# A fused attention and mixture kernel whose feed-forward pieces stand six slots sooner in the written order

## The chip, the cores and the metric

The kernel runs on one core of one Trainium2 chip. The metric is the device time of one execution in microseconds (us). Five engines work side by side, each through its own instructions in order: TensorE (PE in the profile), VectorE (DVE), ScalarE (ACT), GpSimd (POOL) and SyncE (SP), which here only starts transfers. They meet through semaphores.

## The reference

For 32 sequences of 256 tokens with 256 channels, a gated cross attention is added to `x` and then a gated feed-forward part:

```python
x = x + tanh(g_xattn) * xattn(layernorm(x), ctx, ctx, W, b, mask)    # 16 heads, 77 keys, causal and padded
x = x + tanh(g_ffn)   * ffn(layernorm(x), ...)
# ffn: shared = swiglu(flat @ w_in.T) @ w_out.T
#      h      = swiglu(flat @ w1.T); routed = sum over e of (h * w_se[:, e]) @ w2[e].T
#      w_se: of 2 groups the likelier, in it the 2 best of 4 experts (softmax, top 2)
```

## The kernel before

**Two phases.** Phase one computes attention, the second layer norm, the router and the shared feed-forward part, and it sorts tokens by pair of experts: an indirect transfer from GpSimd (L1473) writes each token's record into a table. Phase two gathers the tokens of each pair, tile by tile, and multiplies them with the experts' weights.

**One written order.** `phase_one()` returns a list of entries (name, index, part). Every engine walks through this same list and issues what is its own of each entry, so that the list fixes the order on all queues. The list is made by a loop over steps i = 0 to 34, each of 12 slots. In step i the stages of four batches overlap: the key/score work of batch i-1 (`max`), scores and values of batch i-2, projection and second norm of batch i-3, first norm of batch i. A batch is one sequence of 256 tokens; two batches make a chunk.

**Feed-forward pieces.** The shared part of a chunk is cut into 24 pieces `ffn`, and two of them stand at the end of every odd slot. Pieces 0 to 15 make the hidden layer (L712, three matmuls of 512 columns each), four pieces for each of the four blocks fc of 128 hidden channels. At the second piece of a block ScalarE computes a tanh (L932) and VectorE a product (L1248, "u"); at the fourth VectorE computes the block (L1256, "f"). At the second piece of the *next* block ScalarE rounds f (L853, `gh`) and GpSimd computes the rest f - gh (L1375, `gl`). Pieces 16 to 23 multiply `gh` and `gl` with the output weights (L729, six matmuls of 256 columns each); piece 16 + fc waits for `gl` of block fc. After pieces 19 and 23 VectorE adds the result to x (L1266, `res`) and SyncE stores it (L510).

The wait of the second half of the pieces, and what GpSimd does at an entry `moments` (the inverse root of a variance and a scaled mean, four small instructions L1382, L1384, L1431, L1433, the first of which waits for VectorE's statistics L989 and L993):

```python
if hb == 0:
    e.wait_ge(s["gl"], 4 * b + fc + 1)      # TensorE, pieces 16 to 19
...
root(0, b)                                   # GpSimd at "moments": waits for VectorE, then L1382, L1384
```

**Routing steps.** With each piece one routing step of VectorE (L1032 to L1131) is issued, from the step on at which the chunk's logits are there; steps 30 to 37 of a route are the eight table writes of GpSimd (L1473). A route takes 38 steps and starts in slot 5 of every fourth step. So VectorE has routing steps 8 to 19 in steps 8, 12, ..., 28 and GpSimd has its table writes at the end of step 9, 13, ... and in steps 10, 14, ..., 30.

**Banks.** `take()` gives each use of PSUM a bank of a ring, and the use waits until the one before it in that bank has been read. `max`, `scores` and `att` share two pairs of banks (ring P): the first `scores` of a step (L615) waits until VectorE has read the `att` of the step before (L1212), the k-th `max` (L586) until VectorE has reduced the one before (L1192).

**Transfers of x.** SyncE loads x of a batch for the residual (L500) in slot 11, behind the copies of `queries` (L487), and GpSimd adds the bias (L1449) in slot 2 of the next step; VectorE's projection (L1221) waits for that.

Of the kernel before, what the change touches and what calls it, by code (L numbers as in the profile page):

```python
# [59 lines left out]
def phase_one():  # L60

    order = []
    at = {"ffn": 0, "r": 0, "k": 0}
# [8 lines left out]
    def ffn(routes):  # L72

        order.append(("ffn", pieces[at["ffn"]] // 24, pieces[at["ffn"]] % 24))
        at["ffn"] += 1
        for _ in range(routes):
            route()
# [14 lines left out]
    for i in range(NB + 3):  # L92
        slots = [[] for _ in range(12)]

        def put(b, stages):
            if 0 <= b < NB:
                for slot, name, k in stages:
                    slots[slot].append((name, b, k))

        if i % 2 == 1:  # L100
            put(i - 4, ((2, "logits", 0), (5, "logitsT", 0)))
            if i < NB + 1:
                put(i - 4, ((6, "store_x2", 0),))
        put(i - 2, ((1, "scores", 0), (3, "scores", 1), (5, "scores", 2), (5, "values", 0), (7, "scores", 3), (8, "values", 1),
                    (5 if i < 6 else 11, "load_x1", 0), (11, "att", 0)))

        put(i - 1, ((0, "max", 0), (0, "max", 1), (0, "max", 2), (0, "max", 3), (3, "maxT", 0)) if i < 6 else
            ((0, "max", 0), (2, "max", 1), (4, "max", 2), (6, "max", 3), (9, "maxT", 0)))

        put(i - 3, ((2, "bias", 0), (1, "attT", 0), (4, "proj", 0), (7, "norm2", 0), (10, "x2T", 0)) if i < NB + 2 else  # L110
            ((1, "bias", 0), (1, "attT", 0), (3, "proj", 0), (5, "norm2", 0), (7, "x2T", 0), (9, "logits", 0), (10, "logitsT", 0)))
        put(i, ((2, "norm", 0), (6, "xT", 0), (10, "queries", 0)))
        put(i + 1, ((8, "moments", 0),))

        put(i, ((1, "keys", 0), (3, "keys", 1)))
        if i == 0:
            slots[5].append(("init", 0, 0))
            slots[8].append(("vau", 0, 0))
            slots[9].append(("own", 0, 0))
            slots[11].append(("load_kv", 1, 0))  # L120
        if i == 1:
            slots[8].append(("own", 1, 0))
            slots[10].append(("gates", 0, 0))
            slots[11].append(("masks", 1, 0))
        if i == 2:
            slots[4].append(("zeros", 0, 0))
            slots[6].append(("pads", 1, 0))
            slots[11].append(("load_weights", 0, 0))

        if i == 2:  # L130
            slots[8].append(("weights", 0, 0))
            slots[10].append(("weights", 1, 0))
        if i in (4, 5):
            slots[9].append(("weights", i - 2, 0))

        if i == 5:
            slots[2].append(("weights_low", 2, 0))
        if i == 6:
            slots[1].append(("weights_low", 3, 0))
        if i % 2 == 1 and i + 1 < NB:  # L140
            slots[11] += [("kv", i // 2 + 1, 0), ("vau", i // 2 + 1, 0)]
        if i % 2 == 0 and 0 < i < NB - 2:
            slots[8].append(("load_kv", i // 2 + 1, 0))
        if i == NB:
            slots[0].append(("load_w1", 0, 0))
        if i == NB + 1:
            for k in range(4):
                slots[2 * k + 2].append(("split", k, 0))
        if i == NB + 2:
            order.append(("wide", 0, 0))  # L150
            for k in range(4):
                slots[2 * k + 2].append(("hid", 0, k))
        for slot in range(12):
            for name, b, k in slots[slot]:
                order.append((name, b, k))
                if name == "logitsT":
                    logits.add(b // 2)
            if slot == 3 and i + 2 < NB:
                order.append(("load_x", i + 2, 0))
            while at["ffn"] < (12 * (i - 5) + slot - 9) // 2 * 2:  # L160
                ffn(1 if i < NB - 1 else 3)
            if i == NB + 2 and slot == 4:
                held = None
        if 1 <= i < 5:
            order.append(("clear", i - 1, 0))
# [31 lines left out]
def build(nc, A, out):  # L197
    ctx = ExitStack()
    with ctx:
        order = phase_one()  # L200
        names = (

# [1352 lines left out]
```

How the kernel before makes its waits and increments, by code:

```python
        def sync(e):  # L414
            def load_kv(b):
                h = b % 2
                if b >= 1:
                    e.wait_ge(s["klo"], b)
                e.dma_start(kf[:, :, :], A["ctxT"][b].rearrange("p (a k) -> p a k", k=K)).then_inc(
                    s[f"kf{h}"], 16)
                if b >= 1:
                    e.wait_ge(s["vau"], b)
                e.dma_start(vf[:, :, :], A["ctx_1024"][b * G:b * G + G].rearrange("b k d -> k b d")).then_inc(
                    s[f"vf{h}"], 16)
# [4 lines left out]
                for r, t in enumerate((khi, klo, khi)):  # L429
                    for j in range(2):
                        o = 32 * r + 16 * j
                        dst = Kst[o:o + 16, h, j, :, :, :].rearrange("p q a k -> p (q a k)")
                        e.dma_start(dst.bitcast(F), t[64 * j:64 * j + 64, :, :].bitcast(F)).then_inc(s[f"kd{h}"], 16)
            for stage_, b, k in order:
                h = b % 2
                if stage_ == "load_x":
                    if b >= 2:
                        e.wait_ge(s["xn"], b - 1)
                    e.dma_start(xt[:, h, :, :], A["x"][b].rearrange("(t p) d -> p t d", p=P)).then_inc(
                        s[f"xi{h}"], 16)
                elif stage_ == "consts":
# [11 lines left out]
                    e.dma_start(wt_s, A["WT"].rearrange("(c p) n -> p c n", p=P)).then_inc(s["w2"], 16)  # L454
                elif stage_ == "masks" and b == 1:
                    e.wait_ge(s["ks1"], 2)
# [568 lines left out]
                def after():  # L1026
                    e.wait_ge(*chain[0])
```

## Time and profile before

| | us |
|---|---|
| runs: median of three (lowest, highest) | 1164.55 (1162.37, 1165.7) |
| profiled execution, first to last instruction | 1154.6 |
| TensorE busy in it | 1105.4 |
| VectorE, GpSimd, ScalarE busy | 820.0, 519.1, 470.4 |
| steps 6 to 31 of phase one | from 91.2 to 633.0 |

The profiled execution's own time outside its span is not recorded; the span lies 9.95 us under the median of the runs, which is launch and end. The clock of TensorE was at its upper level (2.4 GHz, 1.0 in the profile) for nearly all of the span, mean 0.987. A row of the timeline gives start, length, engine, line, operation, what it writes and reads, and in brackets how long its engine was idle before it and for whom.

### The profile page before, as it was taken

What the parts mean: (1) busy time and instruction counts of PE and PEld (TensorE: products, weight loads), DVE (VectorE), ACT (ScalarE), POOL (GpSimd) and SP (SyncE); (2) the same over time, 40 slices, a digit from 0 to 9 for tenths busy, and PEclk for the clock granted to TensorE, in tenths of its full rate; (3) what the DMA queues carried; (4) which work ended last, traced back from release to release, by engine and by line L of the source; (5) the groups of instructions that cost most, each with busy time, mean ns of one, the idle gap of its engine ahead of it and who ended that gap; (6) DMA issues with size and microseconds to landing.
All of it is one profiled execution on the core that took longest, in us unless ns stands there. A gap on an engine that the chain in (4) does not pass through costs nothing.

```text
span 1154.6 us, 22482 instructions
## 1 busy us (share of the span) xinstructions
PE 1105.4 (96%) x7475; PEld 917.9 (80%) x7475; DVE 820.0 (71%) x1778; ACT 470.4 (41%) x722; POOL 519.1 (45%) x647
## 2 busy tenths in 40 slices
PE   5789999999999999999999899999999899999997
PEld 3557888787887788788788677788888788888886
DVE  7757686786786876876877576557544588888886
ACT  4565556545555555555654432223221111111111
POOL 5334447347356346456454523100000666666564
PEclk9989999999999999999999999999999899999999
DMA  8984647656665765764755311587662554555451
GB/s 158 242 191 80 145 98 128 132 118 107 136 125 93 148 131 115 123 141 102 118 117 109 70 46 38 199 263 236 209 211 93 162 160 150 164 162 157 147 177 65
DMA packets 106163, 160.65 MB, mean 139 GB/s; under 512 B 28828, under 2 KB 70718, under 8 KB 106048
## 3 DMA queue, kind: packets, MB, share of 16 engines
q1 hardware_dynamic: 94276, 121.18, 46.0%
q0 software_dynamic: 11776, 38.03, 10.6%
q8 instruction: 65, 1.06, 0.4%
q14 instruction: 46, 0.38, 0.1%
HBM read 75.24 MB, written 52.10 MB: 110 GB/s over the span
## 4 chain that ended last, share of the span: by engine, by line
PE 72%; DVE 10%; issue 8%; POOL 6%; ACT 2%; DMA 1%; POOLq 0%; ACTq 0%; DVEq 0%
PE ps L767 15%; PE ps L814 12%; PE ps L712 8%; PE ps L816 6%; PE ps L729 6%; PE ps L632 4%; PE ps L620 3%; PE ps L663 3%; PE ps L799 3%; POOL tab_dram L1473 2%; PE ps L586 2%; PE ps L590 2%; PE ps L615 1%; PE ps L697 1%; PE ps L686 1%
## 5 line engine op out<-in xcount | busy, mean ns | idle before, releaser
L814 PE MATMUL ps<-regr,gh 128*128 x600 | 221.5, 407 | 0.1
L891 ACT ACTIVATE Pt<-ps,pbias 77x1024 f32<-77x1024 f32 x128 | 141.4, 1105 | 107.4 <-PE ps L620 106.2
L816 PE MATMUL ps<-regr,gl 128*128 x600 | 170.0, 283 | 0.0
L814 PEld LDWEIGHTS ps<-regr,gh 128*128 128x128 f32 x600 | 113.8, 190 | 23.6 <-issue 0.5
L981 ACT ACTIVATE gh<-ps 128x512 fp32r<-128x512 f32 x75 | 44.8, 599 | 204.5 <-PE ps L799 204.5
L1192 DVE TENSOR_REDUCE mneg<-ps 128x8 f32<-128x616 f32 x128 | 100.5, 792 | 19.7 <-PE ps L590 19.6
L816 PEld LDWEIGHTS ps<-regr,gl 128*128 128x128 f32 x600 | 114.2, 190 | 0.0
L712 PE MATMUL ps<-x2h,winh 128*128 128x512 f32 x256 | 110.6, 432 | 0.5 <-DVE OHR L1096 0.5
L1375 POOL TENSOR_TENSOR gl<-gf,gh 128x512 fp32r<-128x512 f32 x64 | 82.5, 1290 | 50.4 <-ACT gh L853 50.1
L712 PE MATMUL ps<-x2h,winl 128*128 128x512 f32 x256 | 101.5, 396 | 0.0
L712 PE MATMUL ps<-x2l,winh 128*128 128x512 f32 x256 | 101.2, 395 | 0.0
L1449 POOL TENSOR_TENSOR x<-x,regf 128x512 f32<-128x512 f32 x32 | 41.1, 1284 | 130.4 <-DMA x<-in_x 130.4
L1361 POOL DMA_INDIRECT yt<-y_dram,Pt x73 | 75.5, 1035 | 53.2 <-PE ps L816 42.7
L1499 POOL DMA_INDIRECT out<-ot,Pt x75 | 77.6, 1035 | 41.3 <-issue 27.9
L1287 DVE SCALAR_TENSOR_TENSOR Pt<-Pt,ps 128x512 f32<-128x512 f32 x64 | 44.0, 688 | 69.0 <-ACT Pt L975 67.8
L975 ACT ACTIVATE Pt<-ps 128x512 f32<-128x512 f32 x64 | 38.3, 598 | 129.8 <-PE ps L767 129.8
L620 PE MATMUL ps<-regr 100*77 100x256 f32 x512 | 87.9, 295 | 0.0
L767 PE MATMUL ps<-regr,x2h 128*128 128x512 f32 x256 | 82.4, 396 | 0.0
L1424 POOL TENSOR_TENSOR regr<-regr,own 128x616 fp32r<-128x616 f32 x64 | 78.4, 1226 | 5.7 <-ACT regr L862 5.4
L1473 POOL DMA_INDIRECT tab_dram<-rec,slot x64 | 64.7, 1011 | 26.7 <-issue 13.3
L1320 DVE SCALAR_TENSOR_TENSOR ot<-ps,Pt,ot 128x256 f32<-128x256 f32 x150 | 72.6, 484 | 5.4
L632 PE MATMUL ps<-Pt,regf 77*32 77x256 f32 x1024 | 69.5, 389 | 6.1 <-ACT Pt L891 6.1
(201 smaller groups left out, 2681.7 us busy)
## 6 DMA issues: line engine op xcount, KB each, us to landing
regr<-regr SPq DMA_DIRECT2D x96, 256.0 KB, 5.9
y_dram<-Pt SPq DMA_DIRECT2D x64, 256.0 KB, 2.2
regf<-in_x SPq DMA_DIRECT2D x32, 256.0 KB, 2.9
x<-in_x SPq DMA_DIRECT2D x32, 256.0 KB, 7.2
y_dram<-res SPq DMA_DIRECT2D x32, 256.0 KB, 2.2
regr<-regr SPq DMA_DIRECT2D x96, 77.0 KB, 6.9
x_dram<-x2h SPq DMA_DIRECT2D x14, 512.0 KB, 3.0
x_dram<-x2l SPq DMA_DIRECT2D x14, 512.0 KB, 3.8
```

The source lines that it names most:

```text
L620: m = e.matmul(bk[0:K, j * S:(j + 1) * S], Kst[:, ks, j, p % 4, 2 * g + p // 4, :], Xs[:, h, p % 4, p // 4, :], start=False, stop=j == 1, ...
L632: m = e.matmul(bk[32 * j:32 * j + 32, q * S:(q + 1) * S], Vau[:, ks, g, n, :], Pt[0:K, n, :], start=True, stop=True)
L712: m = e.matmul(bk[:, :], w[:, cc, off:off + P], x[:, b % 2, cc, :], start=cc == 0 and n == 0, stop=cc == 1 and n == 2)
L767: i = e.matmul(bk[:, :], x[:, cc, k * P:(k + 1) * P], w[:, cc, half * 512:half * 512 + 512], start=n == 0, stop=n == 5)
L814: e.matmul(o, gh2[:, k % 3, fc, :], w2v[:, bass.ds(val, 1), fc, :, :].rearrange("p o h d -> p (o h) d"), start=fc == 0, stop=False, skip_g ...
L816: m = e.matmul(o[:, 0, :], gl2[:, k % 3, fc, :], w2v[:, bass.ds(val, 1), fc, 0, :].rearrange("p o d -> p (o d)"), start=False, stop=fc == ...
L891: e.activation(Pt[0:K, 4 * k:4 * k + 4, :].rearrange("k (n j) t -> k n (j t)", n=2), bank_of["sc", b, k][0:K, :, :], ACT.Exp, bias=pbias[: ...
L1192: e.tensor_reduce(mneg[:, h, t, :].rearrange("p (j q c) -> p c j q", j=2, c=2)[:, c], bank_of["mm", b, k][:, :, 0:4 * K].rearrange("p q (f ...
L1375: e.tensor_tensor(gl[:, fc, :], gf[:, n % 2, :], gh[:, fc, :].bitcast(F), ALU.subtract).then_inc(s["gl"], 1)
L1424: e.tensor_tensor(Kbd[:, b % G, k, :, :], khi[:, b % G * 2 + k, :].bitcast(F).unsqueeze(1).broadcast_to([P, 8, K]), own8[:, :].unsqueeze(2 ...
L1473: e.indirect_dma_start(tab, bass.IndirectOffsetOnAxis(ap=slot[:, j:j + 1], axis=0), rec[:, j, :], None, bounds_check=NC * NT - 1, oob_is_e ...
L1499: e.indirect_dma_start(out.rearrange("b s d -> (b s) d"), bass.IndirectOffsetOnAxis(ap=rt[:, k, 0:1].bitcast(I32), axis=0), ot[:, k % 8, : ...
```

## The change

The number of pieces that must have been placed by slot `slot` of step `i` is `(12 * (i - 5) + slot - 9) // 2 * 2` before and `(12 * (i - 5) + slot - 3) // 2 * 2` after. The first two pieces stand in slot 5 of the sixth step (i = 5) instead of slot 11, and each piece after them six slots sooner. The routing steps are tied to pieces, but a route starts when its logits are in the list, which has not moved.

```diff
             if slot == 3 and i + 2 < NB:
                 order.append(("load_x", i + 2, 0))
-            while at["ffn"] < (12 * (i - 5) + slot - 9) // 2 * 2:
+            while at["ffn"] < (12 * (i - 5) + slot - 3) // 2 * 2:
                 ffn(1 if i < NB - 1 else 3)
             if i == NB + 2 and slot == 4:
                 held = None
```

How a chunk c lies in the slots of its steps (odd step 5 + 2c, even step 6 + 2c and so on; each slot named holds two pieces):

| | slots and pieces |
|---|---|
| before | odd 11: 0, 1; even 1: 2, 3; 3: 4, 5; 5: 6, 7; 7: 8, 9; 9: 10, 11; 11: 12, 13; next odd 1: 14, 15; 3: 16, 17; 5: 18, 19; 7: 20, 21; 9: 22, 23 |
| after | odd 5: 0, 1; 7: 2, 3; 9: 4, 5; 11: 6, 7; even 1: 8, 9; 3: 10, 11; 5: 12, 13; 7: 14, 15; 9: 16, 17; 11: 18, 19; next odd 1: 20, 21; 3: 22, 23 |

**GpSimd in an even step without table writes.** The rows run from slot 1 to the end of the step; L1424 are the keys, L1449 the bias, L1382 and L1384 the roots, L1375 is `gl`. Before:

```order
L1424 TENSOR_TENSOR regr<-regr,own 128x616
L1375 TENSOR_TENSOR gl<-gf,gh 128x512
L1382 TENSOR_SCALAR ve<-mv 128x2
L1384 TENSOR_TENSOR rs<-ve,mhalf 128x2
L1442 TENSOR_TENSOR first<-pad,caus 128x77
L1375 TENSOR_TENSOR gl<-gf,gh 128x512
L1382 TENSOR_SCALAR ve<-mv 128x2
L1384 TENSOR_TENSOR rs<-ve,mhalf 128x2
L1431 TENSOR_TENSOR mr<-mv,rs 128x2
L1433 TENSOR_SCALAR mr<-mr 128x2
L1375 TENSOR_TENSOR gl<-gf,gh 128x512
```

After, with what the instructions wait for (s_mom0 is VectorE's statistics of the next batch, s_gh ScalarE's rounding):

```order
L1424 TENSOR_TENSOR regr<-regr,own 128x616
L1382 TENSOR_SCALAR ve<-mv 128x2 [waits s_n2,s_mom1]
L1384 TENSOR_TENSOR rs<-ve,mhalf 128x2 [waits s_ve1]
L1375 TENSOR_TENSOR gl<-gf,gh 128x512 [waits s_gh]
L1442 TENSOR_TENSOR first<-pad,caus 128x77 [waits s_mm]
L1382 TENSOR_SCALAR ve<-mv 128x2 [waits s_xn,s_mom0]
L1384 TENSOR_TENSOR rs<-ve,mhalf 128x2 [waits s_ve0]
L1431 TENSOR_TENSOR mr<-mv,rs 128x2 [waits s_rs0,s_xn]
L1433 TENSOR_SCALAR mr<-mr 128x2 [waits s_mr]
L1375 TENSOR_TENSOR gl<-gf,gh 128x512 [waits s_gh]
```

The `gl` behind L1433 was that of block 2 of the chunk, of which the fourth followed in slot 3 of the next step; now it is that of block 3, the last one.

**TensorE at the end of the same even step after the change** (L673 transposes the second norm, L641 the attention output; behind them pieces 18 and 19):

```order
L673 MATMUL ps<-ident,xn 128x128 [waits s_n2,s_OT]
L673 MATMUL ps<-ident,xn 128x128 x3
L641 MATMUL ps<-ident,regf 128x128 [waits s_mx,s_OT]
L641 MATMUL ps<-ident,regf 128x128 x7
L729 MATMUL ps<-woh,gh 128x256 [waits s_gl]
L729 MATMUL ps<-wol,gh 128x256
```

Before, pieces 12 and 13 (L712, which wait for no `gl`) stood there, and piece 19 stood in slot 5 of the next step.

**VectorE in slots 7 and 8 of such a step** (L1230 is the second norm, L1072 and L1075 are routing steps 14 and 15, L989 and L993 the statistics that L1382 waits for). Before:

```order
L1230 TENSOR_SCALAR xn<-x,mv,rs 128x256
L1072 TENSOR_REDUCE cl<-cs 128x8 [waits s_rv]
L1248 SCALAR_TENSOR_TENSOR tt<-tt,ps 128x512 [waits s_t]
L1075 TENSOR_TENSOR OH<-cl,io 128x96 [waits s_rv]
L989 BN_STATS st<-regf 128x6 [waits s_xn,s_xi1]
```

After:

```order
L1230 TENSOR_SCALAR xn<-x,mv,rs 128x256
L1072 TENSOR_REDUCE cl<-cs 128x8 [waits s_rv]
L1256 TENSOR_TENSOR gf<-tt,ps 128x512 [waits s_gl,s_hb,s_u]
L1075 TENSOR_TENSOR OH<-cl,io 128x96 [waits s_rv]
L989 BN_STATS st<-regf 128x6 [waits s_xn,s_xi1]
```

The product "u" of a block has changed places with the "f" of a block; the routing steps stand where they stood.

## Rows read from the trace of the kernel before

**Rows 1.** The page's first part: busy time of each engine and share of the span

```profile
PE 1105.4 (96%) x7475; PEld 917.9 (80%) x7475; DVE 820.0 (71%) x1778; ACT 470.4 (41%) x722; POOL 519.1 (45%) x647
```

**Rows 2.** Windows: steps 5, 12, 13, 14, a tail stretch; length, busy by engine, clock, DMA

```profile
68.46:91.15 22.69, 20.08 (x126) 15.00 (x125) 14.60 (x32) 11.12 (x17) 8.57 (x13) 0.73 0.74 160
...
215.28:234.93 19.65, 19.38 (x143) 15.30 (x142) 17.23 (x41) 11.59 (x17) 7.68 (x12) 1.00 0.74 123
234.93:257.39 22.46, 22.17 (x189) 18.74 (x188) 18.47 (x45) 11.25 (x17) 9.62 (x16) 1.00 0.51 119
257.39:276.92 19.53, 19.37 (x144) 15.30 (x143) 13.38 (x29) 11.58 (x17) 15.19 (x16) 1.00 0.81 128
...
648.00:660.02 12.02, 9.39 (x59) 7.35 (x53) 4.51 (x9) 4.68 (x9) 7.93 (x9) 0.86 0.20 27
```

**Rows 3.** Waits of TensorE from 91 to 633 us: total, times, longest

```profile
PE ps L615 <- DVE regf L1212: 2.9, 10, 0.3
PE ps L586 <- DVE mneg L1192: 2.1, 7, 0.6
PE ps L673 <- DVE xn L1230: 0.7, 2, 0.5
```

**Rows 4.** Timeline, end of step 12: POOL, DVE and PE

```profile
230.91 1.30 POOL L1375 TENSOR_TENSOR gl<-gf,gh 128x512 fp32r<-128x512 f32 x1 [2.56 <-ACT gh L853]
...
234.79 0.24 POOL L1433 TENSOR_SCALAR mr<-mr 128x2 f32<-128x2 f32 x1
...
230.95 1.37 DVE L1075 TENSOR_TENSOR OH<-cl,io 128x96 bf16<-128x96 f32 x1
...
233.02 0.25 DVE L993 BATCH_NORM_AGGREGATE mv<-st 128x2 f32<-128x6 f32 x2
...
234.24 0.39 PE L712 MATMUL ps<-x2h,winh 128*128 128x512 f32 x1
...
234.93 0.45 PE L586 MATMUL ps<-regr 128*128 128x308 f32 x2
```

**Rows 5.** Timeline, step 14: POOL, then the start of PE's last piece

```profile
265.97 1.28 POOL L1449 TENSOR_TENSOR x<-x,regf 128x512 f32<-128x512 f32 x1 [2.53 <-DMA x<-in_x]
...
278.75 0.24 POOL L1433 TENSOR_SCALAR mr<-mr 128x2 f32<-128x2 f32 x1
278.95 1.28 POOL L1375 TENSOR_TENSOR gl<-gf,gh 128x512 fp32r<-128x512 f32 x1
...
276.22 0.39 PE L712 MATMUL ps<-x2h,winh 128*128 128x512 f32 x1
```

**Rows 6.** Timeline of DVE at 630 us: the routing step of rows 4 again

```profile
630.77 0.25 DVE L1075 TENSOR_TENSOR OH<-cl,io 128x96 bf16<-128x96 f32 x1
```

**Rows 7.** Timeline, end of step 11 and start of step 12: ACT, DVE, PE

```profile
213.22 0.60 ACT L913 ACTIVATE x2h<-ps 128x512 fp32r<-128x512 f32 x1 [1.30 <-PE ps L673]
...
215.48 0.60 ACT L932 ACTIVATE tt<-ps 128x512 f32<-128x512 f32 x1 [1.18 <-PE ps L712]
...
214.84 0.75 DVE L1212 TENSOR_TENSOR regf<-ps,rden 128x256 f32<-128x256 f32 x2
...
215.85 0.30 PE L615 MATMUL ps<-cauT,identb 77*77 77x154 bf16 x2
```

**Rows 8.** Timeline of PE in step 5: the wait in it, a hidden-layer matmul

```profile
84.33 1.93 PE L632 MATMUL ps<-Pt,regf 77*32 77x256 f32 x16 [1.29 <-ACT Pt L891]
...
90.10 0.63 PE L712 MATMUL ps<-x2h,winh 128*128 128x512 f32 x1
```

**Rows 9.** Timeline of PE in step 32: the longest wait of the tail

```profile
653.26 0.63 PE L673 MATMUL ps<-ident,xn 128*128 128x128 f32 x4 [2.62 <-DVE xn L1230]
...
656.40 0.63 PE L712 MATMUL ps<-x2h,winh 128*128 128x512 f32 x1
```

**Rows 10.** Timeline of SP's queue in step 11: two issues ahead of the load of x

```profile
211.94 0.68 SPq L490 DMA_DIRECT2D regr<-regr  x1
213.56 0.37 SPq L510 DMA_DIRECT2D y_dram<-res  x1
```

## The prediction

> **What bounds the kernel now.** I read the page's busy times first: TensorE is busy for 1105.4 of 1154.6 us [rows 1]. The reader is to see that almost no idle time is left to win. Next, the windows: steps 12, 13 and 14 last 19.65, 22.46 and 19.53 us and TensorE is busy for all but 0.27, 0.29 and 0.16 us of them, at the full clock [rows 2]. The third view is the list of TensorE's waits over steps 6 to 31, 542 us: its three largest entries are 2.9, 2.1 and 0.7 us [rows 3]. So in steady state TensorE is the bound, and the others reach it just in time. The permuted pieces are the same matmuls, so nothing is won on the work itself; the change can only move waits. Two places have idle time to fill: step 5 (busy 20.08 of 22.69 us, mean clock 0.73) and the stretch around step 32 (9.39 of 12.02 us) [rows 2].
>
> The last view was the timeline of the even steps, since a piece has two kinds of cover: what TensorE does between a block's last hidden piece and the piece that multiplies it. Before, pieces 15 and 19 of a chunk are separated by slots 2 to 5 of an odd step (logits, two `max`, two `scores`, projection, values). After, they are separated by slots 8 to 11 of an even step, which hold only values, small transposes and three pieces. In the same time VectorE must make f, ScalarE gh and GpSimd gl, and GpSimd now has the four instructions of `moments` ahead of that gl, which wait for VectorE's statistics.
>
> **The change part by part.** Instructions are neither added nor removed. My sum is made in differences on the profiled execution (1154.6 us of span) and put on the median of the runs, 1164.55 us, since the 9.95 us between them (launch and end) are untouched.
>
> *Piece 19 in even steps with routing (steps 8, 12, ..., 28; six).* In step 12 GpSimd ends L1433 at 234.79 + 0.24 = 235.03. The last piece of the step, where piece 19 will stand, starts at 234.24 [rows 4]. The gl behind L1433 takes 1.30 us and about 0.05 us of signalling, so it would end at 236.4: a wait of 2.1 us on TensorE. VectorE's part of this chain shifts. Block 3's u now stands in slot 5 and must wait for a tanh of 0.60 us [rows 7] that f at that place did not need; with the `max` behind it I put this at +1.0 us. Against it stands L1075, which took 1.37 us while gl ran from 230.91 to 232.21 [rows 4] and 0.25 us where it was alone [rows 6]. After the change no gl stands at that place, which gives 1.12 us back. Together 2.0 us, from 1.0 (only the L1075 saving comes) to 3.1 (L1075 stays at 1.37). Six times: **+12.0 us** (6 to 19).
>
> The page "SBUF — State Buffer" of the Trainium skill, section "Who interferes with whom", says that a VectorE instruction with two SBUF inputs and a GpSimd instruction that reads SBUF cannot run together; whichever comes second waits for the whole of the first. The trace agrees with it: the L1075 of 1.37 us ends with that gl. If it did not hold and 1.37 us were L1075's own length, the term would be 6 x 3.1 = 18.6 us instead of 12.0.
>
> *Piece 19 in even steps with table writes (10, 14, ..., 30; six).* GpSimd is the late one here: busy for 15.19 of 19.53 us in step 14 [rows 2]. L1433 ends at 278.99, 2.77 us after the last piece of the step has started [rows 5]. In the stretch from slot 9 of the odd step to that point there is one gl more after the change (three instead of two): +1.31. The wait of 2.53 us for the load of x [rows 5] goes, because GpSimd comes to it later and the load starts sooner. That leaves 1.55 us, plus 1.35 for the gl behind: 2.9, less 0.4 by which TensorE itself is later (next term): 2.5 us. Low end 1.2 (only VectorE's chain counts), high end 4.1 (two thirds of the transfer wait stays). Six times: **+15.0 us** (7 to 25).
>
> *Step 6.* No routing: GpSimd is some 1.2 us better placed than in step 12, **+1.0 us** (0 to 1.4).
>
> *First `scores` of the even steps (13).* In step 11 ScalarE rounds x2 at 213.22, VectorE ends L1212 at 215.59, and L615 starts at 215.85, which is 0.26 later; where TensorE does wait for L1212 it starts 0.13 after its end. After the change slot 9 of the odd step holds pieces 4 and 5, so a tanh (0.60) and a rounding (about 0.6) stand ahead of that rounding of x2 and end near 213.8, and L1212 ends 0.55 later. TensorE waits 0.42 us [rows 7]. 13 x 0.42 = **+5.5 us** (0 to 12). What is queued behind L615 is the whole step, the exponentials on ScalarE first.
>
> *Waits that go.* VectorE gets time at the start of each odd step while TensorE waits at piece 19, so the 2.9 us of L615 and the 0.7 us of L673 go; the 2.1 us of L586 stay, since VectorE's order there costs the same [rows 3]. **-3.6 us.**
>
> *Load of x.* In step 11 the store of `res` (issued at 213.56) holds back `queries` and the load of x on SyncE's queue; without it they could follow the issue that ends at 211.94 + 0.68 = 212.62, so some 1.4 us sooner [rows 10]. This frees VectorE's projection and is hidden work on GpSimd and VectorE: 0 us by itself, counted in the terms above and in the tail.
>
> *Start.* Step 5 gets six more pieces. A piece takes 234.93 - 234.24 = 0.69 us [rows 4] at the full clock, so 4.2 us of TensorE's work leave the end of the kernel. They fill the 1.29 us wait before L632 at 84.33; the rest lengthens the step, at twice the length as long as the clock is at 1.2 GHz (0.63 us for a matmul at 90.10 against 0.39) [rows 4, 8]. If the clock stays low as long as before, 0.3 us is gained; if the fuller TensorE gets 2.4 GHz back after the first stretch, 3.4 us. I take **-2.0 us**.
>
> *Tail.* In step 32 TensorE waits 2.62 us for the second norm, which waits for GpSimd's root behind six table writes and the late bias of batch 29; then the clock is at 1.2 GHz for a while, which costs some 1.4 us on two pieces (a matmul of 0.63 us for 0.39) [rows 4, 9]. With the load sooner by about 2 us and one gl fewer between bias and root, both go: -4.0. Piece 19 waits there as well: +1.2. **-2.8 us** (-4 to +2).
>
> Sum: 12.0 + 15.0 + 1.0 + 5.5 - 3.6 - 2.0 - 2.8 = +25.1, so 1164.55 + 25.1 = 1189.7, say 1190 us.
>
> **The rivals.**
> *A: gl comes in time, and the kernel gets faster.* The sooner load of x and the missing contention speed up GpSimd and VectorE so far that block 3's gl ends before piece 19. Then only the gains stand: -3.6 - 2.0 - 4.0 = -9.6, so 1155 us. It decides where L1433 ends 1.35 us or more before TensorE reaches piece 19. For it speaks that GpSimd is idle for 2.56 us before a gl in step 12 [rows 4]; against it that L1433 ends 0.79 and 2.77 us after that point now, so 2.1 and 4.1 us would have to be won, and only 1.1 and 2.5 us are in sight. Chance 0.08.
> *B: nothing measurable happens.* TensorE is the bound, the pieces are only permuted, the waits are covered by the list of matmuls it holds: 1162 to 1167 us. The covers of 0.1 to 0.3 us in the steady state speak against it. Chance 0.05.
> *C: as forecast, and the clock falls too.* In step 32 a wait of 2.62 us was followed by a stretch at 1.2 GHz [rows 9]; the waits of 2.5 us that I expect in six steps are nearly as long, and each stretch would cost 1.4 us or more, some also behind the 2.0 us waits: +8 to +15, so 1198 to 1205. Against it: steps 1 to 5 have many small waits and few low stretches. Chance 0.20.
> The forecast itself, waits at piece 19 at the full clock: 0.67, its own range 1176 to 1198.
>
> The page "TensorE: Matmul & The Clock Gate", section "Why this matters for your kernels", advises to avoid idle gaps of about 3 us between matmuls; no run here yet shows waits of just that length.
>
> **How the numbers follow.** The low ends of the terms give about +8, the high ends over +40 with the clock. Rivals A and B lie below 1168, C reaches to 1205. A range of 1170 to 1203 leaves out A, B and a sliver of C and of the forecast's ends, some 0.2. Within 0.3% (3.5 us) is what a measurement of this kernel can hardly tell from no change: B and a little of the others, 0.05. Faster: A, 0.08. Slower: 0.87.
>
> **What would show it.** In the changed profile TensorE's waits should have a new first entry, L729 on gl L1375, some 13 to 14 times, 1 to 3 us each and about 28 us in all, in even steps only. The even steps should last about 22 us instead of 19.6, the odd ones as before or 0.3 us less. L1075 should have 0.25 us instead of 1.37. L615's waits should move from odd to even steps. L673's wait in step 32 should be gone, and step 5 with its six more pieces should last 23 to 26 us. I am wrong if L729 has no wait (rival A or B), or if the mean clock falls clearly below 0.98 (rival C).

## The result, and the profile after

| | before | after |
|---|---|---|
| median of 6 runs each, same chip, us | 1164.04 (1162.37 to 1165.7) | 1218.59 (1215.22 to 1221.79) |
| profiled execution: span, time, us | 1154.6 (span) | 1217.8, 1219.49 |
| mean granted clock of the profiled execution, share of full speed | 0.987 | 0.978 |

The ratio is 1.047, 95% interval 1.0446 to 1.0495: the change makes the kernel 54.5 us slower. The forecast was 25 us slower, in a range that ended at 1203 us. The direction was right, the size less than half of what came, and the time lies outside the range.

The first part of the page after, which answers to [rows 1]:

```profile
PE 1122.9 (92%) x7475; PEld 922.8 (76%) x7475; DVE 829.9 (68%) x1778; ACT 467.7 (38%) x722; POOL 521.6 (43%) x647
```

The number of instructions is the same on every engine, so nothing was added. TensorE's busy time grew by 17.5 us for the same 7475 matmuls. The same matmuls at the same clock would be as busy as before, so this growth points to a stretch at the lower clock.

TensorE's waits of the kernel after from 95 us (start of step 6) to 668 us (end of step 30), which answer to [rows 3]; the columns are total, number and longest, in us:

```profile
PE ps L729 <- POOL gl L1375: 24.0, 13, 2.2
PE ps L673 <- DVE xn L1230: 7.8, 6, 1.3
PE ps L586 <- DVE mneg L1192: 5.7, 7, 0.9
PE ps L615 <- DVE regf L1212: 3.8, 13, 0.3
PE ps L598 <- DVE regr L997: 2.5, 6, 0.4
PE ps L574 <- DVE x L1221: 1.2, 3, 0.6
```

The first line is the forecast wait: 13 times, in the even steps. The five lines under it come to 21.0 us, where before they and all others came to under 7. Of these only L615's was in the forecast.

Windows of the kernel after: steps 5, 12, 13, 14, 15, and the stretch at the end of step 14. The columns are length, busy time (and instructions) of PE, PEld, DVE, ACT and POOL, the granted clock, the share of the DMA engines and GB/s, as in [rows 2]:

```profile
69.70:94.95 25.25, 22.43 (x145) 17.38 (x144) 15.00 (x32) 13.71 (x21) 7.67 (x13) 0.86 0.61 127
230.51:253.90 23.39, 20.18 (x155) 15.85 (x154) 19.12 (x45) 11.57 (x17) 11.80 (x16) 1.00 0.70 105
253.90:275.80 21.90, 21.90 (x179) 18.18 (x178) 14.87 (x40) 11.23 (x17) 5.81 (x11) 1.00 0.47 121
275.80:300.39 24.59, 20.46 (x155) 16.32 (x154) 16.04 (x32) 11.34 (x17) 21.42 (x25) 0.98 0.82 110
300.39:322.82 22.43, 22.43 (x168) 18.66 (x168) 13.11 (x34) 11.48 (x19) 6.02 (x10) 0.94 0.38 109
299.61:303.02 3.41, 3.41 (x18) 3.05 (x18) 1.55 (x2) 0.22 (x1) 0.70 (x1) 0.52 0.91 166
```

Step 12 went from 19.65 to 23.39 us, of which TensorE idles 3.2. Step 14 went from 19.53 to 24.59, of which it idles 4.1. The odd steps hold other matmuls than before (six pieces moved forward), so they are compared in groups of four steps: 83.5 us before, 92.3 after. Step 15 shows a second thing that the forecast did not have. TensorE is busy for all of it, and yet the clock is 0.94; the last line has the reason, 3.4 us at about half clock, on either side of the boundary between steps 14 and 15. Such a stretch stands at the end of each of the six steps 10, 14, ..., 30 (from 207.3, 299.5, 391.7, 483.8, 576.0 and 668.1 us); before there was none between 91 and 654 us.

The timeline of the kernel after at the end of step 12, which answers to [rows 4]: POOL, then PE and DVE.

```profile
244.44 1.30 POOL L1375 TENSOR_TENSOR gl<-gf,gh 128x512 fp32r<-128x512 f32 x1 [1.46 <-ACT gh L853]
...
250.14 0.22 POOL L1382 TENSOR_SCALAR ve<-mv 128x2 f32<-128x2 f32 x1 [4.13 <-DVE mv L993]
...
251.57 0.24 POOL L1433 TENSOR_SCALAR mr<-mr 128x2 f32<-128x2 f32 x1
251.77 1.26 POOL L1375 TENSOR_TENSOR gl<-gf,gh 128x512 fp32r<-128x512 f32 x1
...
253.09 0.38 PE L729 MATMUL ps<-woh,gh 128*128 128x256 f32 x1 [1.61 <-POOL gl L1375]
...
231.32 1.58 DVE L1148 TENSOR_TENSOR regr<-regf,regr 128x308 fp32r<-128x308 f32 x1
...
244.48 1.34 DVE L1069 TENSOR_TENSOR cs<-s,io 128x64 f32<-128x64 f32 x1
...
248.85 0.25 DVE L1075 TENSOR_TENSOR OH<-cl,io 128x96 bf16<-128x96 f32 x1
```

This is the place that the forecast priced at 2.0 us. GpSimd sits idle for 4.13 us on the statistics of VectorE, does the four steps of `moments`, and only then the gl that TensorE waits for, 1.61 us. The last two DVE lines show what the forecast missed. L1075 is short now, as it said, because no gl runs beside it. But a gl (that of block 2) now runs at 244.44, together with L1069, which takes 1.34 us. L1148, at the start of the step, takes 1.58 us. The same instructions in the kernel before, in step 12, and L1230 of step 14, which is needed below:

```profile
215.51 0.47 DVE L1148 TENSOR_TENSOR regr<-regf,regr 128x308 fp32r<-128x308 f32 x1
...
227.58 0.21 DVE L1069 TENSOR_TENSOR cs<-s,io 128x64 f32<-128x64 f32 x1
...
273.30 0.74 DVE L1230 TENSOR_SCALAR xn<-x,mv,rs 128x256 f32<-128x256 f32 x2 [1.50 <-POOL rs L1384]
```

The timeline at the end of step 14, which answers to [rows 5]: POOL, then DVE and PE.

```profile
291.15 0.73 POOL L1384 TENSOR_TENSOR rs<-ve,mhalf 128x2 f32<-128x2 f32 x1
292.06 1.07 POOL L1473 DMA_INDIRECT tab_dram<-rec,slot  x1 [0.19 <-issue]
293.16 1.27 POOL L1375 TENSOR_TENSOR gl<-gf,gh 128x512 fp32r<-128x512 f32 x1
...
297.68 0.24 POOL L1433 TENSOR_SCALAR mr<-mr 128x2 f32<-128x2 f32 x1
297.88 1.25 POOL L1375 TENSOR_TENSOR gl<-gf,gh 128x512 fp32r<-128x512 f32 x1
...
291.98 2.61 DVE L1230 TENSOR_SCALAR xn<-x,mv,rs 128x256 f32<-128x256 f32 x2 [0.41 <-POOL rs L1384]
...
294.74 0.63 PE L673 MATMUL ps<-ident,xn 128*128 128x128 f32 x4 [1.29 <-DVE xn L1230]
...
299.19 0.39 PE L729 MATMUL ps<-woh,gh 128*128 128x256 f32 x1 [2.24 <-POOL gl L1375]
...
299.75 0.41 PE L729 MATMUL ps<-woh,gh 128*128 128x256 f32 x1
```

There are two waits here. L1230 normalizes x in two instructions; in this step the pair takes 2.61 us (the second alone 2.29, where its shortest is 0.41) and is over when the gl behind the table write is over. TensorE waits 1.29 us for it, does 2 us of work, and waits 2.24 us for the last gl. After this second wait the matmuls of L729 take 0.41 us instead of 0.28: this is the low clock.

**Where the 63.2 us between the two spans arose.** Up to step 6: 3.9 (step 5 holds six more pieces). Steps 6 to 30: 54.2. Step 31: 3.3. Step 32 up to the second phase: -2.2. First part of the second phase: 4.0. The 54.2 us are the difference of the waits in the list (+39.3: 24.0 on gl, 7.1 on L673, 3.6 on L586, 0.9 on L615, 2.5 on L598, 1.2 on L574), plus six low stretches (about 8, see `gl_first` below), plus what a wait costs beyond its row. From one start of a matmul to the next, piece 19 lost 1.78 us in step 12 where the row says 1.61, and 2.40 in step 14 where it says 2.24. With about 29 waits more than before at 0.16 each this is 4.6. Some 2 us of the 54.2 stay unassigned.

### The profile page after: what moved, and what is told of

Same layout as the page of the kernel before. It is cut to its first block, busy times and chain, and to the rows that moved or that the text cites. A ratio compares the mean times of both kernels' runs of the same rounds, so it can differ in the third digit from the quotient of the medians.

```text
span 1217.8 us, 22482 instructions
## 1 busy us (share of the span) xinstructions
PE 1122.9 (92%) x7475; PEld 922.8 (76%) x7475; DVE 829.9 (68%) x1778; ACT 467.7 (38%) x722; POOL 521.6 (43%) x647
## 4 chain that ended last, share of the span: by engine, by line
PE 66%; DVE 13%; POOL 10%; issue 8%; ACT 3%; DMA 1%; POOLq 0%; ACTq 0%; DVEq 0%
PE ps L767 15%; PE ps L814 12%; PE ps L712 7%; PE ps L816 6%; PE ps L729 5%; PE ps L620 3%; PE ps L632 3%; POOL tab_dram L1473 3%; PE ps L663 3%; PE ps L799 3%; POOL gl L1375 2%; PE ps L586 2%; DVE xn L1230 2%; PE ps L590 2%; POOL rs L1384 2%
## 5 line engine op out<-in xcount | busy, mean ns | idle before, releaser
L1382 POOL TENSOR_SCALAR ve<-mv 128x2 f32<-128x2 f32 x64 | 15.0, 235 | 248.9 <-DVE mv L993 248.4
L1375 POOL TENSOR_TENSOR gl<-gf,gh 128x512 fp32r<-128x512 f32 x64 | 82.4, 1290 | 77.2 <-ACT gh L853 76.8
L1192 DVE TENSOR_REDUCE mneg<-ps 128x8 f32<-128x616 f32 x128 | 100.1, 790 | 20.5 <-PE ps L590 20.5
L712 PE MATMUL ps<-x2h,winh 128*128 128x512 f32 x256 | 108.9, 425 | 0.8 <-DVE gf L1256 0.8
L712 PE MATMUL ps<-x2h,winl 128*128 128x512 f32 x256 | 101.6, 397 | 0.0
L729 PE MATMUL ps<-woh,gh 128*128 128x256 f32 x256 | 78.5, 307 | 24.7 <-POOL gl L1375 24.7
L712 PE MATMUL ps<-x2l,winh 128*128 128x512 f32 x256 | 101.3, 396 | 0.0
L1248 DVE SCALAR_TENSOR_TENSOR tt<-tt,ps 128x512 f32<-128x512 f32 x64 | 43.7, 682 | 71.3 <-ACT tt L932 70.5
L1424 POOL TENSOR_TENSOR regr<-regr,own 128x616 fp32r<-128x616 f32 x64 | 78.4, 1226 | 0.2 <-issue 0.2
L586 PE MATMUL ps<-regr 128*128 128x308 f32 x256 | 64.4, 335 | 13.3 <-DVE mneg L1192 9.5
```

The lines of the kernel that those rows point to most:

```text
L586: e.matmul(o[:, q], xTh[:, h, c, t * P:(t + 1) * P], Kbd[:, g, c, 4 * q:4 * q + 4, :], start=True, stop=False)
L712: m = e.matmul(bk[:, :], w[:, cc, off:off + P], x[:, b % 2, cc, :], start=cc == 0 and n == 0, stop=cc == 1 and n == 2)
L729: m = e.matmul(o[:, t, :], x[:, fc, at:at + P], w[:, fc, :], start=fc == 0 and t == 0 and n == 0, stop=fc == 3 and n == 2, skip_group_chec ...
L1192: e.tensor_reduce(mneg[:, h, t, :].rearrange("p (j q c) -> p c j q", j=2, c=2)[:, c], bank_of["mm", b, k][:, :, 0:4 * K].rearrange("p q (f ...
L1375: e.tensor_tensor(gl[:, fc, :], gf[:, n % 2, :], gh[:, fc, :].bitcast(F), ALU.subtract).then_inc(s["gl"], 1)
L1424: e.tensor_tensor(Kbd[:, b % G, k, :, :], khi[:, b % G * 2 + k, :].bitcast(F).unsqueeze(1).broadcast_to([P, 8, K]), own8[:, :].unsqueeze(2 ...
```

## The experiments

I had two theories of the 54 us. **W**: it all hangs on the order on GpSimd, that is on gl standing behind `moments`; the other waits and the low clock follow from it. **C**: a good part is contention between VectorE and GpSimd, that is gl and the table writes now run at times when VectorE's next result is on the path. Ratios below are to the kernel before, run on the same chip beside each batch.

**gl_first: GpSimd does the gl of the last hidden block ahead of `moments`.** Only GpSimd's own order is changed.

```diff
+            mine = list(order)
+            for n in range(len(order)):
+                if order[n][0] == "moments":
+                    for m in range(n + 1, n + 8):
+                        if order[m][0] == "ffn" and order[m][2] == 17:
+                            mine[n:m + 1] = order[n + 1:m + 1] + [order[n]]
-            for stage_, b, k in order:
+            for stage_, b, k in mine:
```

> The changed kernel, but on GpSimd alone the entry `moments` of an even step stands behind the gl of block 3 instead of ahead of it. Theory W (piece 19 waits for that gl behind `moments`; 24.7 us of waits in the changed profile and a low clock after six of them): the waits of L729 go, about 25 us plus 8 us of low clock, so 1183 to 1190 us. Rival P (GpSimd is simply too full, whichever order): the wait moves to the norm of the next batch or to the table writes, and less than 10 us is won: 1209 or more. By theory C (VectorE blocked by GpSimd at L1230, L1148, L1069) some 15 to 20 us of the loss must stay in any case, so not under 1180.

Measured: 1185.68 us, ratio 1.0225 (1.0168 to 1.0282); of the 54 us 33 are gone by the medians, 28 by the ratios. TensorE's waits from 95 to 630 us (steps 6 to 30 end at 636 us here, so the last even step is cut off):

```profile
PE ps L673 <- DVE xn L1230: 6.5, 5, 1.3
PE ps L586 <- DVE mneg L1192: 5.6, 7, 0.9
PE ps L615 <- DVE regf L1212: 3.5, 12, 0.3
PE ps L598 <- DVE regr L997: 2.5, 6, 0.4
PE ps L729 <- POOL gl L1375: 1.6, 5, 0.3
```

The wait on gl falls from 24.0 to 1.6 us (1.9 with the last step), and the others stay. So W is right for the wait that was forecast, and wrong in that the others follow from it. The windows of its steps 14 and 15:

```profile
265.79:288.06 22.27, 20.08 (x155) 15.93 (x154) 16.02 (x32) 11.43 (x17) 19.68 (x22) 1.00 0.77 109
288.06:309.32 21.26, 21.26 (x168) 17.69 (x167) 13.06 (x35) 11.48 (x19) 7.76 (x14) 1.00 0.50 127
```

The clock is 1.00 in both. Step 15, which holds the same matmuls, takes 21.26 us instead of 22.43; with the 0.15 or so in the last matmuls of step 14 a low stretch costs 1.3 us, six of them about 8. The 22 us of waits and the 8 of clock account for what was gained. The wait of 1.3 us on L673 is still there and did not lower the clock by itself.

**gl2_small: the gl of block 2 cut to 8 of 512 columns** (the product of the rest uses old values). It is cut from the second chunk on; it is the gl behind the table write in step 14.

```diff
-                e.tensor_tensor(gl[:, fc, :], gf[:, n % 2, :], gh[:, fc, :].bitcast(F), ALU.subtract).then_inc(s["gl"], 1)
+                w = 8 if b and fc == 2 else 512
+                e.tensor_tensor(gl[:, fc, 0:w], gf[:, n % 2, 0:w], gh[:, fc, 0:w].bitcast(F), ALU.subtract).then_inc(s["gl"], 1)
```

> The changed kernel with the gl of block 2 cut to 8 of 512 columns (from the second chunk on; the rest of that block's low part is then stale). Theory C: L1230 in steps 10, 14, ... falls from 2.3 to 1.1 us or less and L1069 in steps 8, 12, ... from 1.34 to 0.22; TensorE's waits before the second norm's transposes (1.45) and before maxT (0.78) go, and with GpSimd 1.3 us earlier the wait at piece 19 of steps 10, 14, ... shrinks by about 1: in all 15 to 25 us, so 1194 to 1204. Rival W alone: only the wait at piece 19 shrinks, 6 to 8 us, so 1210 to 1213.

Measured: 1197.56 us, ratio 1.0284 (1.0248 to 1.032), 21 us less than after: C's figure. The timeline at the same place of step 14:

```profile
289.10 1.06 POOL L1474 DMA_INDIRECT tab_dram<-rec,slot  x1 [0.19 <-issue]
290.20 0.22 POOL L1376 TENSOR_TENSOR gl<-gf,gh 128x8 fp32r<-128x8 f32 x1
...
289.02 0.78 DVE L1230 TENSOR_SCALAR xn<-x,mv,rs 128x256 f32<-128x256 f32 x2 [0.40 <-POOL rs L1385]
```

L1230 takes 0.78 us instead of 2.61, beside the same table write. So it was gl that held it, for longer than gl itself runs, and L673's wait is gone from the list. L1069 takes 0.24 us instead of 1.34, and L598's wait is gone with it. The wait on gl before piece 19 stays at 2.4 us in these steps (in steps 8, 12, ... it falls to 1.0), and three of the six low stretches are gone (steps 10, 22 and 30 keep theirs). In my expectation I had both waits of these steps shrink; that was wrong.

**shift4 and shift2: pieces four and two slots sooner instead of six.** The constant 3 of the changed line becomes 5 and 7 (9 was before).

```diff
-            while at["ffn"] < (12 * (i - 5) + slot - 3) // 2 * 2:
+            while at["ffn"] < (12 * (i - 5) + slot - 5) // 2 * 2:
```

> Pieces four slots sooner than before instead of six (constant 5 for 3). Piece 19 stands in slot 1 of the odd step, behind max, scores and attT of the next step: 2.9 us more of cover than in slot 11. Theory W: no wait on gl in steps 8, 12, ..., 1 us in steps 10, 14, ...: 1168 to 1182 us. Rival C (what costs is where a gl meets VectorE): no step between four and six slots, time between 1175 and 1215 as the coincidences fall.

> Pieces two slots sooner than before (constant 7 for 3). Piece 19 stands in slot 3 of the odd step with even more cover. Theory W: no wait on gl at all, 1160 to 1168 us, with 1 or 2 us won at the start. Rival C: some coincidence may cost 5 to 15 us here as well.

Measured: shift4 1162.36 us, ratio 0.9997 (0.9975 to 1.002); shift2 1164.53 us, ratio 1.0011 (0.999 to 1.0032). `shift4` lies below both of its expectations, `shift2` within W's. The price is a step, not a slope: with four slots the wait on gl is 2.5 us in six waits, with two slots there is none. What decides on that wait, by these two and `gl_first`, is whether piece 19 falls into the stretch of the even step where GpSimd has `moments` ahead of gl. The two also differ in contention. With four slots L1230, L1069 and L1148 take 0.4, 0.22 and 0.47 us and L1075 takes 1.37, as before. With two slots the second L1230 takes 2.0 to 2.3 us and L1069 takes 1.33, as with six, and TensorE still has no wait at L673 (only 0.4 us at L598, six times). So the same hold on VectorE costs nothing there: it costs where TensorE's next work is that result.

**shift8: eight slots sooner** (constant 1).

> Pieces eight slots sooner than before (constant 1 for 3). The gl of block 3 stands in slot 7 of the even step, ahead of `moments`; piece 19 in slot 9, so the cover is shorter than with six slots (values, maxT, two pieces). Theory W (the order on GpSimd costs, more than the cover): waits on gl of 1 us or less per chunk, 1170 to 1190 us, faster than six slots. Rival D (the shorter cover costs): waits over 2 us per chunk, 1215 or more.

Measured: 1195.92 us, ratio 1.0256 (1.0225 to 1.0286). It moves further and loses less. In its step 12 gl runs ahead of `moments`, as W says:

```profile
242.12 1.27 POOL L1375 TENSOR_TENSOR gl<-gf,gh 128x512 fp32r<-128x512 f32 x1 [2.88 <-ACT gh L853]
...
244.54 0.22 POOL L1382 TENSOR_SCALAR ve<-mv 128x2 f32<-128x2 f32 x1 [1.15 <-DVE mv L993]
```

Its steps 8, 12, ..., 28 have no wait on gl at all. In those with table writes gl has the writes ahead of it and a short cover, and the wait is 3.9 to 4.2 us, once a step. So W's forecast (waits of 1 us or less, 1170 to 1190 us) failed in every second chunk, where rival D's long waits came, and the time lies between the two.

**first_gl2: gl_first and gl2_small together; first_gl2_klo: L1148 also cut to 8 of its 77 columns in each of four parts.** The second edit:

```diff
-                    e.tensor_tensor(klo[:, :, :], kf[:, :, :], khi[:, :, :].bitcast(F), ALU.subtract).then_inc(s["klo"], 1)
+                    w = 8 if b >= 2 else K
+                    e.tensor_tensor(klo[:, :, 0:w], kf[:, :, 0:w], khi[:, :, 0:w].bitcast(F), ALU.subtract).then_inc(s["klo"], 1)
```

> Both edits together on the changed kernel: gl of block 3 ahead of `moments` on GpSimd, and the gl of block 2 cut to 8 columns (its low part is then stale). Theory W + C: the two losses are apart, so from 1185.7 us the wait for the second norm (1.46) goes in six steps, the wait at maxT (0.5) in six, that at piece 19 (0.48) in six: 12 to 16 us, 1169 to 1174 us. Rival (one cause seen twice: GpSimd too full): no more than 5 us, 1181 or more.

> As first_gl2, and VectorE's L1148 (the low part of the keys) cut to 8 columns, so that GpSimd can hold it up no more (its output is then wrong from the third pair on). It took 1.58 us for 0.47 in steps 8, 12, ..., and TensorE waited 1.05 us for the reduction behind it. Theory C: those waits go, 6 to 8 us more than first_gl2, 1162 to 1167 us. Rival (the wait comes from the order, u behind a tanh in slot 1): 1 to 3 us more.

Measured: 1178.62 us, ratio 1.0104 (1.0079 to 1.013), and 1175.4 us, ratio 1.0074 (1.0045 to 1.0103). The two causes add: 1.0225 falls by 0.0121, or 14 us, as expected of it. (The kernel before ran at 1166 us beside this batch and at 1162 beside `gl_first`, so the medians differ by 7 only, and 1178.62 is above the 1169 to 1174 expected.) The second edit is worth 0.0030 or 3.5 us, and the two intervals overlap. It did not do what it was made for: the instruction, L1149 here, is still held by GpSimd's product beside it, and takes 1.28 us with 8 columns where it took 1.57 with all:

```profile
221.81 1.28 DVE L1149 TENSOR_TENSOR regr<-regf,regr 128x32 fp32r<-128x32 f32 x1
...
221.83 1.21 POOL L1432 TENSOR_TENSOR regr<-regr,own 128x616 fp32r<-128x616 f32 x1
```

So the 3.5 us do not price the hold on L1148. TensorE still loses 0.75 us from start to start to the `max` of L1192 in such a step (0.87 before the edit by its row, 0.59 after it). VectorE's order, the other account of this wait, is unchanged in `gl_small` below. There GpSimd's product is nearly over when L1148 starts, L1148 takes 0.48 us, and the row of that wait falls to 0.23:

```profile
220.03 0.48 DVE L1148 TENSOR_TENSOR regr<-regf,regr 128x308 fp32r<-128x308 f32 x1
```

This speaks for the hold and against the order as the cause of most of L586's wait; no run changed this one thing alone.

**late: GpSimd does the table writes one step later, and first_late: both orders together.** Nothing is left out in either. The added lines of `late` (`R_SCAT` is the routing step of the writes):

```diff
+            for entry in mine:
+                if entry[0] == "route" and entry[1] < 6 and entry[2] >= R_SCAT:
+                    moved.append([12, entry])
+                    continue
+                left.append(entry)
+                if entry[0] == "ffn":
+                    for m in moved:
+                        m[0] -= 1
+                    while moved and moved[0][0] <= 0:
+                        left.append(moved.pop(0)[1])
```

> The changed kernel, but GpSimd issues the eight table writes of a route (of the first six routes) 12 pieces, one step, later: in steps 11, 15, ... instead of 10, 14, .... Nothing is left out. Theory W + L (in steps 10, 14, ... GpSimd is late because of the writes): piece 19 there waits 1.2 instead of 2.4 us, the second norm's wait of 1.45 us and the low clock after it go: 20 to 28 us, 1190 to 1198 us. Rival (the writes only move their cost to the odd step): 1210 or more.

> gl of block 3 ahead of `moments` and the table writes one step later, both on GpSimd alone; nothing is left out. If the two causes add: from 1185.7 us another 12 to 16, 1169 to 1175 us. What stays is the order in the even step (max 1, maxT) and the first scores. Rival (the writes meet VectorE elsewhere): 1180 or more.

Measured: late 1199.88 us, ratio 1.032 (1.0272 to 1.0368), 2 us over its 1190 to 1198; first_late 1176.93 us, ratio 1.0132 (1.0083 to 1.018), a little over the 1169 to 1175 expected. In `late` the place of step 14 reads:

```profile
292.86 1.30 POOL L1375 TENSOR_TENSOR gl<-gf,gh 128x512 fp32r<-128x512 f32 x1 [1.18 <-ACT gh L853]
...
295.00 0.72 DVE L1230 TENSOR_SCALAR xn<-x,mv,rs 128x256 f32<-128x256 f32 x2
```

gl is over before L1230 starts, and L1230 takes 0.72 us. The wait on L673 is gone without leaving work out, the wait at piece 19 of these steps is 0.9 us (1.2 in step 10) instead of 2.24, and the low stretches after it are gone. The waits of first_late from 95 to 630 us:

```profile
PE ps L586 <- DVE mneg L1192: 10.1, 10, 1.4
PE ps L615 <- DVE regf L1212: 3.8, 13, 0.3
PE ps L598 <- DVE regr L997: 2.4, 6, 0.4
```

L729 and L673 have left the list; L586 has grown from 5.7 to 10.1. The two largest causes are removed, and a third wait takes part of it back: in most even steps L1148 now takes 1.6 to 2.1 us.

**shift4_first_late: the two orders on GpSimd with four slots**, to see whether a better version lies there.

> The same two edits with pieces four slots sooner instead of six. Four slots alone were as fast as before (ratio 0.9997), with waits of 0.58 us at piece 19 in two of four steps; those go: 1155 to 1162 us where before is 1163, a ratio of 0.994 to 0.999. Rival (TensorE is the bound and nothing is left): 1.000.

Measured: 1163.46 us, ratio 1.0011 (0.9987 to 1.0035). No gain: no version that computes everything beat the kernel before.

**gl_small and before_gl_small: every gl from the second chunk on cut to 8 columns, in the kernel after and in the kernel before.** The edit is that of gl2_small with `w = 8 if b else 512`.

> The changed kernel with all four gl cut to 8 columns from the second chunk on (their low part is stale). GpSimd loses 60 x 1.2 us of work. Theory W: the gl of block 3 still comes behind `moments`, but takes 0.2 instead of 1.3 us: in steps 8, 12, ... some 0.7 us of wait are left, in 10, 14, ... under 1, and the low clock stretches go: 1168 to 1180 us. If the clock and contention were all, it would be 1165 or less; if GpSimd's length of work didn't matter, over 1200.

> Control: the kernel before, with all gl cut to 8 columns from the second chunk on (their low part is stale). By all theories gl's work is hidden there: within 0.4% of before, at most 4 us faster. If it were much faster, the run gl_small would say little about the change.

Measured: gl_small 1165.83 us, ratio 1.0004 (0.9984 to 1.0025); before_gl_small 1149.56 us, ratio 0.9893 (0.9845 to 0.9942). TensorE's waits in gl_small from 95 to 630 us:

```profile
PE ps L615 <- DVE regf L1212: 3.5, 12, 0.3
PE ps L586 <- DVE mneg L1192: 1.8, 7, 0.4
PE ps L729 <- POOL gl L1376: 0.9, 1, 0.9
```

Both lie outside what was expected of them (1168 to 1180 us; at most 4 us faster). With gl_small alone I would have said that gl explains all 54 us. The control forbids it: the kernel before also gains, 13 us where at most 4 were expected. Against their own control the six slots cost 13 us by the ratios (0.0111 of 1163) and 16 us by the spans (1163.5 and 1147.2). So some 38 to 42 of the 54 us hang on gl's time on GpSimd, and 13 to 16 do not. By the spans, of the 16 about 7 arise in steps 6 to 30 (521.4 us against 514.1), where the waits of L615 in the even steps (0.45 in each of 13) come to about 6; some 2 are step 31, and some 7 lie in step 32 and the stretch behind it (92.1 us against 85.0). Why the tail is longer without gl's load was not taken apart.

## Why the prediction was right and wrong

**In short.** The step that failed is the term "Waits that go". It put -3.6 us on the waits of L615 and L673 and nothing on those of L586, L598 and L574, because I asked only where contention of GpSimd and VectorE goes away and not where it comes up. The runs showed 14.4 us more of waits on L673, L586, L598 and L574 instead. Two more terms failed: the clock, put at nothing in the sum (about 8 us), and the tail (9.3 us lost where 2.8 were to be gained).

**Piece 19 in even steps: right.** Forecast were 13 to 14 waits of 1 to 3 us in steps that had none, 28 us in all. There are 15 in the whole run, 24.7 us. With routing a step lost 1.78 against the 2.0 forecast, with table writes 2.40 against 2.5. `gl_first` shows the cause to be the one named, gl behind `moments`. That the size came so near is partly luck. In step 12 GpSimd ended L1433 21.3 us after the start of the step, where the sum had 19.6 (19.75 before, and little change), and TensorE reached piece 19 after 21.0 us, where the sum had 19.0, since it had waited three times on the way. The two errors nearly cancel.

**First `scores` of even steps: right in place, a little large.** All 13 waits are there, 0.3 us each instead of 0.42 (0.45 from start to start); the term was 5.5, and they are 3.8 by the rows. No run tested their cause.

**L1075: right, and behind it the question that was not asked.** It takes 0.25 us, as forecast. But I booked this 1.12 us as saved because "no gl stands at that place", and did not ask where the gl stand after the change, and beside what. In steps 8, 12, ... one stands beside L1069 (1.34 us instead of 0.21). In steps 10, 14, ... one stands beside L1230 (2.61 for the pair instead of 0.72 to 0.78), and L1148 meets GpSimd's copy L1416 and product L1424 (1.58 instead of 0.47). I added up what each VectorE instruction of steps 5 to 31 took over the shortest of its line and shape, where that was over 0.1 us: 29.8 us before, 35.3 after. So the contention grew by some 5 us, and above all it moved. Before, 24 us of it lay on L1075, L1089, L1104 and L1107, and TensorE's list has no wait for them; after, 27 us lie on L1230, L1148 and L1069, and TensorE waits for what comes out of these.

The page "SBUF — State Buffer" of the Trainium skill, section "Who interferes with whom", says that such a conflict holds one engine for the whole instruction of the other, and names `tensor_scalar` among the operations that can take part. The trace agrees on L1069 (1.34 us beside a gl of 1.30). On L1230 it shows more than one gl: the second half was held for 2.29 - 0.41 = 1.88 us, from within the table write to the end of gl (1.27).

**"Waits that go": wrong in sign.** This is the term that the unasked question spoiled. I gave -3.6 us for L615 and L673 and let L586 stay at 2.1. Over steps 6 to 30 L673 rose by 7.1, L586 by 3.6, L598 by 2.5 and L574 by 1.2. The reason given, that VectorE gains time while TensorE waits at piece 19, holds for odd steps alone. The new waits are in the even steps, ahead of piece 19. `gl2_small` and `late` show two ways in which L673's goes away, and `gl2_small` frees L598's with L1069. For L586 the hold on L1148 is the likely cause; L574's wait was not taken apart.

**The clock, rival C: right in kind, too small a chance.** It was priced at 8 to 15 us and given 0.20. Six stretches came, about 8 us in all. I argued from the length of one wait (2.5 us against the 2.62 of step 32). The six steps had two waits, 1.29 and 2.24 us, with 4.4 us between the start of the first matmul after the one and that after the other. Take the second away (`gl_first`) and all six stretches are gone; take the first away (`gl2_small`, one wait of 2.4 us left) and three of the six are. In `shift8` a wait of 3.9 to 4.2 us by itself had such a stretch behind it six times of six. The kernel before has a wait of 2.9 us near its start (L598 at 17.7 us), which I passed over, and the clock stayed at 1.00 behind it. So the length of one wait doesn't decide alone.

**Start: right.** Step 5 lasts 25.25 us, within the forecast 23 to 26. The six pieces are worth 4.2 us and it grew by 2.6, so 1.6 us of its idle time and clock were gained, against 2.0. The steps ahead of it, which the change does not touch, took 1.2 us more in this execution.

**Tail: wrong.** L673's wait in step 32 went, as forecast. In its place stand a wait of 2.2 us of L586 and longer waits for the rank of the routing (L743: 2.6 us at the end of step 31, 1.9 and 0.5 later, 5.0 in all against 2.5 before), and the clock falls once more, for 6.8 us from 739.8. Why these waits came was not tested. From step 31 on the kernel took 5.1 us more, although 4.2 us of pieces had left it: a loss of 9.3 us where 2.8 were to be gained.

**The base: a reading error.** I took the 9.95 us between the profiled span of before and the median for launch and end. The profiled execution after has 1.7 us there (1219.49 and 1217.8). So the profiled execution of before was itself some 8 us quicker than the median run. The forecast was a difference on the median, so its size is not touched, but the spans differ by 63.2 where the medians differ by 54.5.

**The sum.** The spans differ by 63.2 us, 38 more than the forecast's 25.1. Steps 6 to 30 give 24.3 of these: piece 19 came out 4.0 smaller (24.0 against 28) and L615 1.7 smaller (0.9 more than before, against 5.5 - 2.9), L673 was off by 7.8 (7.1 against -0.7), L586, L598 and L574 by 7.3 (against 0), the clock by 8, the restarts by 4.6, and some 2 are unassigned. The tail was off by 12.1 (9.3 against -2.8), the start by 1.6 (-0.4 against -2.0). The medians differ by 8.7 us less than the spans, which is the quick profiled execution of before.

**The range.** It was narrower than the terms under it. Their low ends add up to +2 us (7 + 6 - 3.6 - 3.4 - 4), not "about +8", and their high ends to +55 (19 + 25 + 1.4 + 12 - 3.6 - 0.3 + 2) even without the clock, where 1203 us is +38.5. The result lies at the high ends, although the terms for piece 19 did not: what filled the gap were costs that had no term.

## What to carry to other kernels

When an instruction of an engine that shares a resource is moved, the contention that it causes is moved with it: here its sum grew by some 5 us and the kernel by 54. Look up what stands at the new place as well as what gets free at the old one, and which of the two the bound engine waits for. In an order shared by several in-order engines a move of a few slots costs nothing until the moved work falls behind an instruction that itself waits; then it costs that wait in every step, so find the slot at which it passes before asking how far to move. And run a control: the same work left out of the kernel before showed that a quarter of what "leaving out gl" recovered was not the change's.

## What the runs showed of the hardware

- A VectorE `tensor_scalar` of 128x256 f32 (0.41 us alone) took 2.29 us beside an indirect DMA issue of 1.07 us followed at once by a GpSimd subtraction of 1.27 us. Beside the same DMA issue followed by a subtraction of 8 columns (0.22 us) it was not held (two of them in 0.78 us). Why the hold began before the subtraction's own row is open.
- Two waits of TensorE, 1.29 and 2.24 us, close together, were followed by 3.4 us at a granted clock of 0.52 (most of it at 1.2 GHz), in six steps of six. Single waits of 1.6 us (steps 8, 12, ..., 28), or of 1.3 us alone (`gl_first`), were not. A single wait of 2.4 us was in three steps of six (`gl2_small`), one of 3.9 to 4.2 us in six of six (`shift8`). A stretch of 3.4 us cost 1.3 us.
- A VectorE `tensor_tensor` cut from 128x308 to 128x32 still took 1.28 us beside a GpSimd `tensor_tensor` of 1.21 us (`first_gl2_klo`; 1.57 uncut, 0.47 undisturbed). Making the held instruction small did not free it.
- VectorE's time lost in this way was 29.8 us before and 35.3 after, with 54 us between the kernels. In `shift2` the same hold of 2.0 to 2.3 us on L1230 cost TensorE no wait.
